# Value strips of the second half turned behind all query-key products, from a buffer of their own

## What is computed

```
# x: (4, 96, 128, 128); this is the first of two residual blocks, on group-normed x
xn = _layernorm_c(x, ln_w, ln_b)                       # over the 96 channels
q  = _dwconv3x3(_conv1x1(xn, q_w), q_dw)               # 96 channels
kv = _dwconv3x3(_conv1x1(xn, kv_w), kv_dw)             # 48 channels
k, v = jnp.split(kv, 2, axis=1)                        # 24 and 24
q, k, v -> (b, heads, 12, 128*128), k and v repeated 4 times over the 8 heads
attn = softmax(einsum('bhcn,bhdn->bhcd', _l2norm(q), _l2norm(k)) * temperature)
out  = einsum('bhcd,bhdn->bhcn', attn, v)
x = x + _conv1x1(out, proj_w)
# second block: x + a 1x1 convolution over four convolutions (1x1, 3x3, 5x5, dilated 3x3) of group-normed x
```

## Time and profile before

| | |
|---|---|
| median of 3 runs | 1883.04 us (1882.41 to 1883.69) |
| profiled execution, its own time | 1882.04 us |
| its span, first to last instruction | 1880.3 us |
| TensorE, VectorE, ScalarE, GpSimd busy | 94%, 80%, 55%, 29% |
| mean granted clock of TensorE | 0.974 |
| stage 3, first product to last, four images | 31.10, 31.84, 31.63, 30.21 us |
| stage 4, last product to first L702, four images | 5.48, 5.49, 5.49, 5.49 us |

### The profile page before, as it was taken

One profiled execution on the slowest core, in us unless ns is written; L12 is line 12 of the kernel. 1 busy time (PEld: TensorE's weight loads), 2 busy tenths in 40 slices (PEclk: granted clock), 3 DMA queues, 4 the chain that ended last, 5 costly groups with the idle time before them and its releaser, 6 DMA issues.

```text
span 1880.3 us, 42670 instructions
## 1 busy us (share of the span) xinstructions
PE 1776.1 (94%) x14404; PEld 1690.0 (90%) x14404; DVE 1513.2 (80%) x1974; ACT 1033.0 (55%) x1736; POOL 537.7 (29%) x315
## 2 busy tenths in 40 slices
PE   4999999999999999999999999999999999999997
PEld 3899978999899997999989998899998999799997
DVE  4777678999886648999978655899997765699997
ACT  0756566545285646554546664745536565665551
POOL 5599900222281000123247000022325400003222
PEclk9999989999999998999999999899999999899999
DMA  7012113665501200566630210256661120035553
GB/s 188 0 34 71 30 29 91 157 168 156 143 17 59 71 5 15 132 158 165 171 91 13 70 51 1 50 147 170 160 161 44 35 71 28 1 94 136 130 135 101
DMA packets 101476, 166.83 MB, mean 89 GB/s; under 512 B 40040, under 2 KB 74568, under 8 KB 101224
## 3 DMA queue, kind: packets, MB, share of 16 engines
q1 hardware_dynamic: 77768, 137.72, 29.1%
q10 hardware_dynamic: 23616, 27.94, 4.6%
HBM read 52.86 MB, written 25.17 MB: 41 GB/s over the span
## 4 chain that ended last, share of the span: by engine, by line
PE 41%; DVE 29%; issue 16%; ACT 5%; DMA 3%; SPq 2%; POOL 2%; DVEq 1%; ACTq 1%; POOLq 0%
PE ps L648 11%; PE ps L663 7%; PE ps L665 7%; PE ps L664 7%; DVE region L1289 6%; PE ps L674 6%; DVE region L1223 5%; DVE region L1320 4%; DVE region L1355 3%; ACT region L897 2%; DVE region L1338 2%; DVE region L1230 1%; PE ps L765 1%; DVE region L1234 1%; ACT region L930 1%
## 5 line engine op out<-in xcount | busy, mean ns | idle before, releaser
L765 PE MATMUL ps<-region,W 128*96 128x256 f16 (+4 forms) x7156 | 810.2, 272 | 17.8 <-DVE region L1320 16.7
L765 PEld LDWEIGHTS ps<-region,W 128*96 128x96 f16 (+2 forms) x7156 | 781.1, 123 | 38.4 <-DVE region L1320 22.1
L930 ACT ACTIVATE region<-region 96x1056 f16<-96x1056 f32 (+3 forms) x168 | 208.2, 1284 | 326.6 <-DVE region L1234 298.6
L1145 DVE TENSOR_TENSOR region<-V,band 128x2322 f32<-128x2322 f32 x96 | 261.9, 2731 | 125.0 <-PE ps L665 124.1
L551 POOL TENSOR_TENSOR region<-region,X 96x1536 f32<-96x1536 f32 (+1 forms) x44 | 124.1, 2820 | 587.3 <-DVE region L1355 587.3
L561 POOL TENSOR_TENSOR region<-region 96x1056 f32<-96x1056 f32 (+1 forms) x36 | 85.0, 2361 | 671.9 <-ACT region L911 670.5
L663 PE MATMUL ps<-region 128*128 x1152 | 223.9, 276 | 7.3 <-POOL region L541 6.7
L665 PE MATMUL ps<-region 128*128 x1152 | 222.7, 275 | 0.0
L664 PE MATMUL ps<-region 128*128 x1152 | 222.3, 274 | 0.0
L1320 DVE SCALAR_TENSOR_TENSOR region<-ps,small,region 96x768 f32<-96x768 f32 (+1 forms) x220 | 203.7, 988 | 13.0 <-PE ps L765 10.8
L648 PE MATMUL ps<-proj,region 96*128 96x240 f32 x1024 | 208.0, 366 | 0.0
(11 more groups left out here) (167 smaller groups left out, 2123.0 us busy)
## 6 DMA issues: line engine op xcount, KB each, us to landing
region<-region SPq DMA_DIRECT2D x108, 247.5 KB, 3.8
region<-in_x_dram SPq DMA_DIRECT2D x128, 192.0 KB, 2.3
out_dram<-region SPq DMA_DIRECT2D x40, 576.0 KB, 4.2
region<-region ACTq DMA_DIRECT2D x80, 247.5 KB, 2.4
X<-in_x_dram SPq DMA_DIRECT2D x30, 576.0 KB, 6.1
region<-region SPq DMA_DIRECT2D x36, 247.4 KB, 4.9
X<-in_x_dram SPq DMA_DIRECT2D x19, 384.0 KB, 15.6
region<-region SPq DMA_DIRECT2D x24, 185.6 KB, 3.4
```

Source lines behind the costliest of these rows:

```text
L765: last = mm(o, w, src, start=k == 0, stop=k == len(steps) - 1, skip_group_check=split and ck > 0)
L930: act.activation(dst[0:C, a:e, x:z], src, ACT.Copy).then_inc(s_h, 1)
L1145: v.tensor_tensor(T[:, i].rearrange("p m (i j) -> p m i j", j=3), taps.broadcast_to([P, DM, BW // 3, 3]), mask.broadcast_to([P, DM, BW // ...
```

## The change

The value strips of the second half of an image (`LATE` = 8 strips) get a buffer of their own, `vslate`, with one place for each. It lies exactly where their turned form will be written, in the second half of `vT`: a strip is turned into PSUM first and then evicted over its own source. ScalarE copies all eight of them in a row behind the early strips, with no wait for a free buffer. TensorE's loop over strips is split: its first half is as before, its second has only the query-key products. The transposes of the eight late strips stand behind all products: four before L689, two between L689 and L693, two behind L693 (`late_values`). ScalarE's evictions of them stand two before the root, two between root and exponential, four behind the exponential (`late_values_out`). The warming products are 2, 2 and 1 in place of 7, 5 and 4. VectorE has one memset more, for the pad of `vslate`, behind the present one.

```diff
--- before.py
+++ after.py
@@ -151,6 +151,9 @@
         vT = work[:, 1940:1940 + AT * P]
         S = work[:, 0:2 * GR * QK].rearrange("p (i r c) -> p i r c", i=2, r=GR)
         vs = work[:, 6040:6040 + 2 * GR * VP].rearrange("p (i r c) -> p i r c", i=2, r=GR)
+
+        LATE = GS // 2
+        vslate = work[:, 3988:3988 + LATE * GR * VP].rearrange("p (k r c) -> p k r c", k=LATE, r=GR)
 
         Qf = region[:, 0:WORK]
 
@@ -666,7 +669,20 @@
                         last.then_inc(s_dw, 1)
 
 
-                def gram(g2, first):
+                def turned_values(i, strip, n):
+
+                    pe.wait_ge(s_vs[i], n + 1 + START)
+                    pe.wait_ge(s_vc[i], n + START)
+                    for j in range(GR // 4):
+                        last = tr(ps[:, 1 + i, j * P:(j + 1) * P], strip[:, 4 * j:4 * j + 4, :].rearrange("p r c -> p (r c)"), ident[:])
+                    last.then_inc(s_vt[i], 1)
+
+                def late_values(first, count):
+
+                    for k in range(first, first + count):
+                        turned_values(k % 2, vslate[:, k], b * (GS // 2) + (GS - LATE + k) // 2)
+
+                def gram(g2, first, late):
                     for i in range(2):
                         n = b * (GS // 2) + g2
                         pe.wait_ge(s_S[i], n + 1 + START)
@@ -674,24 +690,25 @@
                             last = mm(ps[0:QK, 0, 0:QK], S[:, i, r, :], S[:, i, r, :],
                                       start=first and i == 0 and r == 0, stop=True, skip_group_check=True)
                         last.then_inc(s_g[i], 1)
-                        pe.wait_ge(s_vs[i], n + 1 + START)
-                        pe.wait_ge(s_vc[i], n + START)
-                        for j in range(GR // 4):
-                            last = tr(ps[:, 1 + i, j * P:(j + 1) * P],
-                                      vs[:, i, 4 * j:4 * j + 4, :].rearrange("p r c -> p (r c)"), ident[:])
-                        last.then_inc(s_vt[i], 1)
-                gram(0, True)
-                with pe.Fori(1, GS // 2) as g2:
-                    gram(g2, False)
-                keep_warm(4, 7)
+                        if not late:
+                            turned_values(i, vs[:, i], n)
+                gram(0, True, False)
+                with pe.Fori(1, (GS - LATE) // 2) as g2:
+                    gram(g2, False, False)
+                with pe.Fori((GS - LATE) // 2, GS // 2) as g2:
+                    gram(g2, False, True)
+                late_values(0, 4)
+                keep_warm(4, 2)
 
                 pe.wait_ge(s_st, sv + N_SCALED + START)
                 st.done(tr(ps[0:QK, 3, 0:QK], att[0:QK, P:P + QK], ident[0:QK, 0:QK]))
-                keep_warm(4, 5)
+                late_values(4, 2)
+                keep_warm(4, 2)
 
                 pe.wait_ge(s_st, sv + N_ATT + START)
                 st.done(mm(ps[:, 3, 0:C], att[0:C, 3 * P:4 * P], pT[:], start=True, stop=True))
-                keep_warm(4, 4)
+                late_values(6, 2)
+                keep_warm(4, 1)
                 for j in range(2):
                     pe.wait_ge(s_vc[j], (b + 1) * (GS // 2) + START)
                 pe.wait_ge(s_st, sv + N_MBLK + START)
@@ -873,22 +890,37 @@
                 pair_of(10, 2)
                 pair_of(11, 0)
                 act.wait_ge(s_qd, (b + 1) * DK + START)
-                with act.Fori(0, GS // 2) as g2:
+                def values(strip, i, g):
+                    act.activation(strip[:, :, 0:KC], Q[:, QK:CO, bass.ds(g * GR, GR)].rearrange("p c r -> p r c"),
+                                   ACT.Copy).then_inc(s_vs[i], 1)
+
+                def values_out(i, g, n):
+                    act.wait_ge(s_vt[i], n + 1 + START)
+                    act.activation(vT[:, bass.ds(g * 2 * P, 2 * P)], ps[:, 1 + i, 0:2 * P], ACT.Copy).then_inc(s_vc[i], 1)
+                with act.Fori(0, (GS - LATE) // 2) as g2:
                     n = b * (GS // 2) + g2
                     for i in range(2):
                         act.wait_ge(s_vt[i], n + START)
-                        act.activation(vs[:, i, :, 0:KC], Q[:, QK:CO, bass.ds((g2 * 2 + i) * GR, GR)].rearrange("p c r -> p r c"),
-                                       ACT.Copy).then_inc(s_vs[i], 1)
+                        values(vs[:, i], i, g2 * 2 + i)
                     for i in range(2):
-                        act.wait_ge(s_vt[i], n + 1 + START)
-                        act.activation(vT[:, bass.ds((g2 * 2 + i) * 2 * P, 2 * P)], ps[:, 1 + i, 0:2 * P], ACT.Copy).then_inc(s_vc[i], 1)
+                        values_out(i, g2 * 2 + i, n)
+                for k in range(LATE):
+                    values(vslate[:, k], k % 2, GS - LATE + k)
+
+                def late_values_out(first, count):
+
+                    for k in range(first, first + count):
+                        values_out(k % 2, GS - LATE + k, b * (GS // 2) + (GS - LATE + k) // 2)
+                late_values_out(0, 2)
 
                 act.wait_ge(s_st, sv + N_DIAG + START)
                 act.activation(col(DIAG, QK), col(DIAG, QK), ACT.Sqrt).then_inc(s_sqrt, 1)
 
+                late_values_out(2, 2)
                 act.wait_ge(s_st, sv + N_NMX + START)
                 act.activation(att[0:C, 2 * P + 32:2 * P + 32 + KC], att[0:C, 2 * P:2 * P + KC], ACT.Exp, bias=col(NMX),
                                accum_out=col(DEN)).then_inc(s_exp, 1)
+                late_values_out(4, 4)
 
                 with act.Fori(0, SETS) as k:
                     act.wait_ge(s_x1, (b * SETS + k + 1) * AR + START)
@@ -1148,6 +1180,7 @@
                 dve.wait_ge(s_qd, (b + 1) * DK + START)
                 dve.wait_ge(s_ns, (b + 1) * AT + START)
                 v.memset(vs[:, :, :, KC:VP], 0.0)
+                v.memset(vslate.rearrange("p k r c -> p (k r) c")[:, :, KC:VP], 0.0)
                 with dve.Fori(0, GS // 2) as g2:
                     for i in range(2):
                         dve.wait_ge(s_g[i], b * (GS // 2) + g2 + START)
```

## The result

| | before | changed |
|---|---|---|
| median of 7 runs beside each other, us | 1883.67 (1879.32 to 1886.63) | 1876.35 (1874.41 to 1881.25) |
| ratio, 95% interval | | 0.996 (0.9945 to 0.9974) |
| profiled execution, us (its span) | 1882.04 (1880.3) | 1874.49 (1872.7) |
| instructions | 42670 | 42406 |

The change makes the kernel faster by 7.3 us, with 4.9 to 10.4 us in the interval. The lines have moved: L674 is L690, the transposes L680 are L677, L884/L887/L890 are L899/L917/L921, L693 is L709, L702 is L719, L1154 is L1187.

A forecast was written before the change was run, and what follows sets the result against it. TensorE was taken to bound the query-key stage, a serial chain over VectorE, ScalarE and TensorE the stage behind it. Strips -5.9, memset +1.6, tail +3.2 gave -1.1 us: forecast 1881.9 us, range 1879.0 to 1886.0.

The forecast's parts named there:

- second memset: VectorE, ahead of the first strip copy: nothing hides its 0.49 us, 0.1 in the first image; +1.6 us in all.
- costs nothing that a row shows: TensorE's strip loop split in two: no cost, since TensorE enters its present loop without a gap.
- The stage behind G: From G, the end of an image's last query-key product, to L702: 6.3 us instead of 5.49; +3.2 us in all.
- saving of 5.9 us: Query-key stage: seven late strips' transposes of 0.21 us leave the path, 1.48 us per image, 5.9 in four.
- pitch 1.68: Late strips on TensorE: they follow each other every 1.68 us instead of 1.89; VectorE's copies allow 1.56.
- rival (f): Late strips: VectorE's copies become the pacer, the 5.9 us don't come, sum up to +4.8, 1887.8 us, slower; chance 0.05.
- (b): ScalarE behind the last query-key product: table load stays by the root, tail +0.4, sum -2.7, 1880.3 us; chance 0.08.
- (a): Tail behind the last query-key product loses nothing, evictions fit beside the chain: -4.3, 1878.7 us, faster; chance 0.05.
- drain of 1.38 us: Skill's rule for ScalarE's table switch: about 1.38 us beside the load, sum 5.5 us higher; the prediction rejected it.
- (e): TensorE drops to 1.2 GHz before L702: +6.8 us, sum +5.7, 1888.7 us, slower; chance 0.08.
- rival (d): First strip of all four images: longer idleness brings 1.2 GHz, +2.8 us, sum 1.7, 1884.7 us; chance 0.14.

The follow-up runs named there:

- one-eviction run: Changed kernel with L719's first set not waiting for late evictions, plus one late eviction instead of two between root and exponential, five behind: one execution, 1879.46 us, no ratio.

## Why the prediction was wrong

**The step that failed** is a term that I had at nothing. My sum has the second memset at the price of its row, and the second block, which the diff leaves alone, at no change; I gave a reason only for TensorE's split loop ("costs nothing that a row shows"), read off one spot where TensorE enters a loop without a gap, and none for VectorE's list. The shown cause of 2.7 us of the gain is that VectorE has one instruction more in its list ahead of the second block: a gap of 0.22 us in every second unit is 0.10 and the first unit is shorter. Removing the instruction brings them back, and another instruction at the start of the kernel takes them away. Why the position in the list matters to VectorE stays open; no view shows it.

**Two terms were too large.** The memset was to cost its row's 0.49 us. Its row is 0.48, yet TensorE's gap grows by 0.1 only. The first copy starts 0.62 us behind the start of the first memset (672.58 to 673.20), where it was 0.35: the issue gap of 0.18 ahead of the copies is gone and the first copy's row begins within the memset's. And the copies take 1.76 for two and not 1.94. Term +0.3, not +1.6. The stage behind G was to cost 0.8 and costs 0.5, because two evictions in a row take 0.66 us and not 0.78, and the first starts at G + 0.42, not 0.53. The load is therefore at G + 2.10 and not 2.37. Term +2.1, not +3.2. With both as measured my sum is -3.5 and the time 1879.5, inside my range, and the 2.7 us of VectorE's list take it to 1876.8; 1876.35 was measured. That these agree within 0.5 us is partly luck, with 2.5 us or more either way on the measured gain.

**What was right.** The saving of 5.9 us, pitch 1.68, TensorE as pacer of the late half, so not rival (f). The load goes with the exponential, so not (b), and the one-eviction run shows that its place in the order sets its time: the exponential is late by 0.18 with four evictions ahead of it and by nothing with three. L719 waits for the last eviction, so not (a). The load's row lasts 1.28 us and the exponential starts 0.02 behind its end, so nothing is paid beside it. The Trainium skill ("ScalarE: Activation LUTs", What ACT_TABLE_LOAD costs) has a drain of 1.38 us there; the measurement decides against it for this kernel. No low clock between G and L719 (both windows 1.00), so not (e); it did come once with fewer warming products alone, in one image of four. At the first strip it is low in the same two of four images; the repeats of the kernel before and of the changed one have four and three such images, so in these traces rival (d)'s 2.8 us is a difference from one execution to the next, and nothing shows that the 0.1 us more of idleness makes it.

**Accounted for:** 3.5 us by the strips and 2.7 by VectorE's list, both as the timelines show them, 6.2 of 7.3 with an interval from 4.9 to 10.4. The ratios agree with each part but would allow much more or less of it. That TensorE's list changes as well is shown; that it is worth nothing here is only as sure as 0.9997 with 0.0013 either way.

## What to carry to other kernels

When an edit inside a large loop adds or removes instructions on an engine, compare stages that it does not touch before crediting it with the whole difference, and run its placement alone (one idle instruction more or less on that engine). Here it alone was worth 2.7 us by the timelines, 0.14%. Work moved into the idle time of a serial chain costs where it delays the next step of that chain: count what each engine's queue has ahead of the step, and make the consumer wait for only what it reads first, which started it 0.57 us earlier in each image here.

## What the hardware showed unexpectedly

- One more instruction in VectorE's list (more than one was not tried), ahead of the images or in them, changes waits of VectorE on its own results hundreds of us later (0.22 or 0.10 us ahead of L1276 in every second unit, 0.47 or 0.11 in the first).
- 128 more instructions on TensorE, 1.74 us of work, cost 12.8 us: at the end of each image it stands up to 2.89 us in one gap with no releaser. A packet of q8 starts 0.3 us into the first of these gaps; that it is the cause is not shown.
- Behind a shorter idle stretch of TensorE (0.57 or 0.93 us in place of 2.00) the last unit is 1.6 us shorter because the clock stays at 2.4 GHz, and the low clock then shows up more often some 10 us later, at the change of image; the ratio was 0.9997.
- A fetch (q8) beside a transfer goes with a late landing: with one 2 to 3 us ahead of the product that reads the transfer, TensorE waited 0.68 to 1.72 us for it in 40 of 40 images, and without one in none of 40.
- Fewer warming products let the next stage start 0.5 us earlier in each image and did not make the kernel faster; in one image of four the clock fell ahead of that stage, which took 0.9 us more.
